# Cross-attention and feed-forward block on one Trainium2 core: the softmax of the first two tiles placed ahead of V and U, and the centring of Wq moved to ScalarE and GpSimd

## The chip, the core and the metric

The kernel runs on one core of a Trainium2 chip. The metric is the device time of one execution in microseconds (us), lower is better. One profiled execution gives the trace; its span runs from the first to the last instruction, and the execution's own time lies somewhat above it. The engines are TensorE (PE; its weight loads are PEld), VectorE (DVE), ScalarE (ACT), GpSimd (POOL) and SyncE (SP), which only issues transfers here.

## What is computed

```python
# x (2, 1024, 256), ctx (2, 77, 192); 8 heads of 128
def xattn(x, ctx):                      # x is layer-normalised first
    q = (x @ Wq) * SCALE; k = (ctx @ Wk) * SCALE; v = ctx @ Wv   # per head
    attn = softmax(q k^T)               # 1024 x 77 per head
    return (attn v) @ Wo + bo
def ffn(x):                             # x is layer-normalised first
    shared = square(relu(x @ Ws1)) @ Ws2
    prob = trunc(softmax(top2(x @ Wr)))     # 8 experts, two chosen
    return shared + routed(x, W1, W2, prob)
x = x + xattn(layernorm(x), ctx)
x = x + ffn(layernorm(x))
```

A truncated softmax weight is 0 unless one of the two is 1, so the routed experts count only where a gate opens. The kernel tests this at its end and runs them in a branch that is not taken with these inputs.

## The kernel before, in words

**Folding.** The kernel multiplies weights with the context first. K and V (transposed, per head) come from the context by `context_main` (rows 0 to 127 of the 192) and `context_tails` (the other 64). Per head h, A = Wq_h K_h^T (256 x 154, both batches) and UT = (V_h Wo_h)^T. Scores of a tile of 128 rows are then x A for 8 heads x 77 keys, in two halves of 308 columns, and attention's output is P U, where U is UT turned. The layer norm's mean is taken out of Wq ahead of time: each row of Wq^T has its mean over the 256 inputs subtracted (`centre_wq`, lines 1039 to 1047), and the row's standard deviation enters as the scale of the exponential. In the same way `wsr_c` is Ws1 and Wr with their mean (`wmean_bank`) subtracted.

**Precision.** A float32 matmul of scores or attention is made of three products of high and low parts (`three`, lines 420 to 422). The high part is a rounded copy by ScalarE (`a_hi`, `u_hi`, `pt_hi`) or GpSimd (`xt_hi`); the low part is a subtraction by VectorE (`a_lo`, `u_lo`, `pt_lo`) or GpSimd (`xt_lo`). So before attention of a tile its probabilities are normalised (GpSimd, `normalise`), turned by TensorE (`transposes`), copied by ScalarE and subtracted by VectorE.

**Tiles.** There are 16 tiles of 128 rows; even ones belong to batch 0, odd ones to batch 1 (`par`). Every engine has its own instruction stream, written by hand, with counting semaphores between them. `step(t)` on TensorE is: turn tile t's probabilities, scores of tile t+2, turn the attended rows of t-1, feed-forward products of t-1 and t-2, attention of t. On ScalarE it is: copies of the turned blocks, the second half of the exponentials of t+1, relu, the first half of those of t+2. Steps 2 to 13 are loops (`pairs`); step 1 and all before are written out.

**The opening.** TensorE makes K, then A (`make_a`) with V's products between the heads, scores of tiles 0 and 1, UT (`make_ut`), U (`make_u` in four parts of two chunks and a last chunk of 104 rows, `last_bank`), part of the scores of tile 2, turns tile 0, the rest of tile 2's scores and one of four parts of tile 3's, attention of tile 0, step 1. VectorE centres Wq two heads at a time (sum, scale, subtract), subtracts A's low parts (`lo_of_a`), makes statistics, maxima and their negation for the exponentials, copies UT, and subtracts U's low parts. ScalarE copies K, A, V, then makes 16 exponentials of tiles 0 and 1 (one per head, lines 691 to 699), then copies U and tile 0's turned probabilities, then tile 2's.

**PSUM.** There are eight banks: `s_ps` four (two per parity, for scores), `g_ps` two (turned blocks), `o_ps`, `f_ps`. In the opening, K and A use the four of `s_ps` (A twice over: head h+4 waits until head h is split), V, UT and U use the other four (`once_banks`), and `last_bank` is the fourth of `s_ps`. Tile 0 is turned into `g_ps` and so waits for U's first parts to be split (line 577 on).

**Transfers.** All loads are issued from SyncE in one queue, in the order: context and Wk, Wq pairs 0 and 1, first half of Wv, Wq pairs 2 and 3, second half of Wv, x_t and x of the first four tiles, Ws1 and Wr, Wo, bo, Ws2, the other x_t and x.

## Time and profile before

| | us |
|---|---|
| median of the three runs shown | 118.31 |
| lowest, highest | 118.0, 119.46 |
| the profiled execution's own time | 118.02 |
| its span | 116.2 |
| busy: TensorE, VectorE, ScalarE, GpSimd | 109.9, 90.1, 84.6, 63.4 |

The granted clock of TensorE is 0.993 of full speed over the span. A row of a timeline gives start and length in us, engine, line, operation, what it writes and reads with shapes, and in square brackets how long the engine had been idle before it and what ended that. Float32 matmuls show as two rows each, transposes and float32r matmuls as one.

### The profile page before, as it was taken

To read this page: it belongs to the slowest core of one execution; us is meant where nothing else is said; L and a number is where in the kernel's file an instruction comes from. 1 tells how busy PE (TensorE), PEld (TensorE's weight loads), DVE (VectorE), ACT (ScalarE), POOL (GpSimd) and SP (SyncE) were. 2 spreads that over 40 slices of the span, in tenths; PEclk is the share of its full clock that TensorE was granted. 3 is DMA by queue.
4 is the path that set the end of the run, shared out by engine and by line. 5 is a ranking of instruction groups with operands and counts; after the bars stand their busy time and mean duration, and the time that the engine had idled before them with its cause. 6 is when DMAs were issued, how large, how long until landed. Compare 5 with 4: busy or idle time off the path is not lost.

```text
span 116.2 us, 3116 instructions
## 1 busy us (share of the span) xinstructions
PE 109.9 (95%) x854; PEld 106.1 (91%) x854; DVE 90.1 (77%) x351; ACT 84.6 (73%) x345; POOL 63.4 (55%) x103
## 2 busy tenths in 40 slices
PE   6997999999899989999999999999999999989981
PEld 6986989998798889999999999999999999979970
DVE  0039987996978597887979797887979696798963
ACT  4016544899659879898989899898989789994320
POOL 2000173359616965786676578657746865369250
PEclk9999999999999999999999999999999999999997
DMA  3799999994000100022005000400400050031033
GB/s 65 249 343 351 352 338 351 351 348 159 0 8 0 71 19 0 6 102 78 0 0 181 0 0 36 145 0 0 177 4 0 0 181 6 0 120 60 29 140 102
DMA packets 11815, 12.70 MB, mean 109 GB/s; under 512 B 1056, under 2 KB 10272, under 8 KB 11808
## 3 DMA queue, kind: packets, MB, share of 16 engines
q1 hardware_dynamic: 11520, 12.36, 32.1%
q10 hardware_dynamic: 288, 0.26, 0.7%
q8 instruction: 3, 0.05, 0.2%
q14 instruction: 4, 0.03, 0.1%
HBM read 8.42 MB, written 2.10 MB: 91 GB/s over the span
## 4 chain that ended last, share of the span: by engine, by line
PE 67%; DVE 12%; ACT 10%; DMA 4%; issue 3%; SPq 2%; DVEq 0%; ACTq 0%
ACT probs L695 8%; PE o_ps L420 7%; PE o_ps L422 7%; PE o_ps L421 7%; PE s_ps L420 6%; PE s_ps L422 6%; PE s_ps L421 6%; PE g_ps L479 5%; PE f_ps L509 4%; DMA wqt_sb<-in_wq_t 4%; PE s_ps L414 3%; PE g_ps L492 2%; PE f_ps L420 2%; DVE row_max L911 2%; DVE u_lo L1032 2%
## 5 line engine op out<-in xcount | busy, mean ns | idle before, releaser
L695 ACT ACTIVATE probs<-s_ps,neg_max,rstd 128x77 f32<-128x77 f32 x128 | 51.5, 424 | 8.8 <-DVE neg_max L919 8.7
L815 POOL TENSOR_TENSOR probs<-probs,recip 128x308 f32<-128x308 f32 x31 | 21.7, 701 | 23.7 <-DVE recip L925 23.7
L695 ACT ACTIVATION_READ_ACCUMULATOR probs<-s_ps,neg_max,rstd 128x1 f32 x128 | 27.3, 213 | 0.0
L420 PE MATMUL o_ps<-u_hi,pt_hi 128*128 128x256 f32 (+1 forms) x80 | 22.7, 284 | 0.9 <-DVE pt_lo L933 0.5
L422 PE MATMUL o_ps<-u_lo,pt_hi 128*128 128x256 f32 (+1 forms) x80 | 22.3, 279 | 0.0
L421 PE MATMUL o_ps<-u_hi,pt_lo 128*128 128x256 f32 (+1 forms) x80 | 22.3, 279 | 0.0
L420 PE MATMUL s_ps<-a_hi,xt_hi 128*128 128x308 f32 x64 | 22.0, 344 | 0.0
L422 PE MATMUL s_ps<-a_lo,xt_hi 128*128 128x308 f32 x64 | 19.5, 304 | 0.0
L421 PE MATMUL s_ps<-a_hi,xt_lo 128*128 128x308 f32 x64 | 19.4, 303 | 0.0
L420 PEld LDWEIGHTS o_ps<-u_hi,pt_hi 128*128 128x128 f32 (+1 forms) x80 | 15.0, 188 | 1.5 <-DVE pt_lo L933 0.9
L421 PEld LDWEIGHTS o_ps<-u_hi,pt_lo 128*128 128x128 f32 (+1 forms) x80 | 15.1, 189 | 0.0
L422 PEld LDWEIGHTS o_ps<-u_lo,pt_hi 128*128 128x128 f32 (+1 forms) x80 | 15.0, 188 | 0.0
L952 DVE TENSOR_TENSOR x_tr<-o_ps,xb_sb 128x256 f32<-128x256 f32 x14 | 5.9, 423 | 9.7 <-PE o_ps L422 9.7
L911 DVE TENSOR_REDUCE row_max<-s_ps 128x8 f32<-128x616 f32 x16 | 12.4, 775 | 0.7 <-PE s_ps L422 0.7
L797 POOL TENSOR_TENSOR xt_lo<-xt_sb,xt_hi 128x256 fp32r<-128x256 f32 x16 | 11.6, 728 | 2.2 <-POOL xt_hi L795 0.2
L420 PEld LDWEIGHTS s_ps<-a_hi,xt_hi 128*128 128x128 f32 x64 | 12.1, 189 | 0.2 <-issue 0.2
L421 PEld LDWEIGHTS s_ps<-a_hi,xt_lo 128*128 128x128 f32 x64 | 12.2, 190 | 0.0
L422 PEld LDWEIGHTS s_ps<-a_lo,xt_hi 128*128 128x128 f32 x64 | 12.0, 188 | 0.0
L819 POOL TENSOR_TENSOR xb_sb<-x_sb,bo_sb 128x256 f32<-128x256 f32 x16 | 11.8, 739 | 0.0
L479 PE MATMUL g_ps<-ident,probs 128*128 128x128 f32 x76 | 11.5, 273 | 0.2 <-POOL probs L815 0.2
L937 DVE TENSOR_TENSOR pt_lo<-g_ps,pt_hi 128x512 fp32r<-128x512 f32 x14 | 9.6, 687 | 1.0 <-ACT pt_hi L681 0.6
L479 PEld LDWEIGHTS g_ps<-ident,probs 128*128 128x128 f32 x76 | 8.7, 140 | 0.5 <-POOL probs L815 0.5
(163 smaller groups left out, 253.4 us busy)
## 6 DMA issues: line engine op xcount, KB each, us to landing
xt_sb<-in_x_t SPq DMA_DIRECT2D x8, 256.0 KB, 6.4
x_sb<-in_x SPq DMA_DIRECT2D x8, 256.0 KB, 6.5
x_sb<-x_tr SPq DMA_DIRECT2D x7, 256.0 KB, 2.3
out<-y_sb SPq DMA_DIRECT2D x6, 256.0 KB, 2.3
wqt_sb<-in_wq_t SPq DMA_DIRECT2D x4, 256.0 KB, 5.1
wo_sb<-in_wo SPq DMA_DIRECT2D x1, 1024.0 KB, 8.8
...
```

The lines of the kernel that those rows point to most:

```text
L420: pe.matmul(out_ap, hi, rhs_hi, start=first, stop=False)
L421: pe.matmul(out_ap, lo, rhs_hi, start=False, stop=False)
L422: return pe.matmul(out_ap, hi, rhs_lo, start=False, stop=last)
L479: mm = pe.transpose(to, probs[:, par, c * P:(c + 1) * P], ident[:, :])
L509: mm = pe.matmul(f_ps[:, D:D + NL], g_sb[:, c * P:(c + 1) * P], wsr_c[:, c, :], start=c == 0, stop=c == DCH - 1)
L695: e = act.activation(probs[:, par, h * TK:(h + 1) * TK], s_ps[:, 2 * par + half, (h - half * H // 2) * TK:(h - half * H // 2 + 1) * TK], A ...
L797: pool.tensor_tensor(xt_lo[:, par, :, :], src, xt_hi[:, par, :, :].bitcast(F32), ALU.subtract).then_inc(xt_ready, 1)
L815: pool.tensor_tensor(rows, rows, recip[:, par, hs].unsqueeze(2).broadcast_to([P, H // 2, TK]), ALU.mult).then_inc(probs_ready, 1)
L819: pool.tensor_tensor(xb_sb[:, par, :], x_sb[:, t, :], bo_sb[:, :], ALU.add).then_inc(xb_ready, 1)
L911: dve.tensor_reduce(row_max[:, par, :].rearrange("p (i h) -> p i h", i=2), s_ps[:, 2 * par:2 * par + 2, 0:HALF].rearrange("p i (h k) -> p ...
L937: dve.tensor_tensor(pt_lo[:, 0:PB], g_ps[:, 0:PB], pt_hi[:, 0:PB].bitcast(F32), ALU.subtract).then_inc(ptlo_ready, 1)
L952: dve.tensor_tensor(x1_of(t, par), o_ps[:, 0:D], xb_sb[:, par, :], ALU.add).then_inc(x1_ready, 1)
```

## The change

- **Wq.** VectorE keeps only the sum and the scale, now by -1/256 (`mean_of_wq`; heads 0 and 1 apart, then pairs). The mean is added by ScalarE for heads 0, 4 and 5 (an Identity with a bias, `centre_wq`) and by GpSimd for heads 1, 2 and 3, 6 and 7 (three instructions), each with a semaphore of its own.
- **A** has eight banks instead of four twice over, so no head waits for a split.
- **Order.** Scores of tiles 0 and 1 come ahead of V, scores of tile 2 ahead of UT. ScalarE makes tile 0's exponentials ahead of V's copies, and tile 2's first half ahead of all of U's.
- **Tile 0** is turned ahead of U, into `s_ps` banks 0 and 2 instead of `g_ps`. Its probabilities and tile 1's have a buffer of their own, `probs_first`, so that tile 2's exponentials don't wait for it.
- **U** is made in the order (0,0), (1,0), (0,1), (1,1) of (batch, half). Attention of tiles 0 and 1 waits for each part of U where it is used, not for all at once.
- **Tile 3's scores**: half of them stand ahead of attention of tile 0 (before: one part of four), the other half in step 1.
- **Transfers.** Wv goes behind x, Ws1 and Wr.

```diff
+        probs_first = sb("probs_first", [P, 2, KC * P])
...
-        a_banks = [s_ps[:, i, :] for i in range(4)] * 2
+        a_banks = [s_ps[:, i, :] for i in range(4)] + once_banks
         u_bank = {(0, 0): once_banks[0], (0, 1): once_banks[1], (1, 0): once_banks[2], (1, 1): once_banks[3]}
         last_bank = s_ps[:, 3, :]
-        wmean_bank = once_banks[2]
+        wmean_bank = once_banks[0]
...
+        def probs_of(t):
+
+            return probs_first if isinstance(t, int) and t < 2 else probs
+
+        def first_one(t):
+            return isinstance(t, int) and t == 0
+
+        def main_turned(t):
+            return s_ps[:, 0, 0:PB] if first_one(t) else g_ps[:, 0:PB]
+
+        def last_turned(t, n):
+            return s_ps[:, 2, 0:n] if first_one(t) else g_ps[:, LO:LO + n]
+
         def pt_bank(t, par, c):
 
+            if first_one(t):
+                return s_ps[:, 0, c * P:(c + 1) * P]
...
-            load_wq(0)
-            load_wq(1)
-            load_wv(0)
-            load_wq(2)
-            load_wq(3)
-            load_wv(1)
+            for i in range(4):
+                load_wq(i)
...
             sp.dma_start(wsr_sb[:, :, 0:FE], ws1.rearrange("(c p) f -> p c f", p=P)).then_inc(wsr_in, 16)
             sp.dma_start(wsr_sb[:, :, FE:NL], wr.rearrange("(c p) e -> p c e", p=P)).then_inc(wsr_in, 16)
+            load_wv(0)
+            load_wv(1)
             sp.dma_start(wo_sb[:, :, :], wo.rearrange("(h p) d -> p h d", p=P)).then_inc(wo_in, 16)
...
-            def make_a(heads):
-                for h in heads:
-                    pe.wait_ge(wq_ready, h // 2 + 1)
+            def make_a():
+                for h in range(H):
+                    if h in (0, 4, 5):
+                        pe.wait_ge(wqact_ready, (1, 2, 3)[(0, 4, 5).index(h)])
+                    else:
+                        pe.wait_ge(wqpool_ready, {1: 1, 2: 2, 3: 2, 6: 3, 7: 3}[h])
                     if h < H // 2:
                         pe.wait_ge(kt_copied, h + 1)
-                    else:
-                        pe.wait_ge(alo_ready, h - H // 2 + 1)
...
-                if isinstance(t, int) and t < 2:
-                    pe.wait_ge(ulo_ready[t], 2)
-                    pe.wait_ge(ulastlo_ready, 1)
                 pe.wait_ge(ptlo_ready, pt_count(t, 0))
                 for c in range(KC):
+                    if isinstance(t, int) and t < 2 and c % 2 == 0:
+                        if c < KC - 1:
+                            pe.wait_ge(ulo_ready[t], c // 2 + 1)
+                        else:
+                            pe.wait_ge(ulastlo_ready, 1)
...
                     if isinstance(t, int) and t == 1:
-                        parts = ((0, 1), (1, 0), (1, 1))
+                        pe.wait_ge(ulastlo_ready, 1)
+                        scores(t + 2, par, ((1, 0),))
+                        transposes_x1(t, par, mm)
+                        scores(t + 2, par, ((1, 1),))
                     else:
-                        parts = ((0, 0), (0, 1), (1, 0), (1, 1))
-                    scores(t + 2, par, parts[:1])
-                    transposes_x1(t, par, mm)
-                    scores(t + 2, par, parts[1:])
+                        scores(t + 2, par, ((0, 0),))
+                        transposes_x1(t, par, mm)
+                        scores(t + 2, par, ((0, 1), (1, 0), (1, 1)))
...
-            make_a(range(0, 4))
-            context_main(wv_sb, 0, wv_in[0], once_banks)
-            make_a(range(4, 6))
-            context_main(wv_sb, 1, wv_in[1], once_banks)
-            make_a(range(6, H))
-            context_tails(wv_sb, once_banks, vt_ready)
-            scores(0, 0)
+            make_a()
+            scores(0, 0, ((0, 0), (0, 1)))
             pe.wait_ge(wsr_in, 32)
-            pe.wait_ge(vt_copied, 3)
+            pe.wait_ge(alo_ready, H // 2 + 1)
             for c in range(DCH):
                 mm = pe.matmul(wmean_bank[:, 0:NL], mean_of[:, :], wsr_sb[:, c, :], start=c == 0, stop=c == DCH - 1)
             mm.then_inc(wmean_ready, 1)
+            scores(0, 0, ((1, 0), (1, 1)))
             scores(1, 1)
+            pe.wait_ge(wsr_ready, 1)
+            for i in range(2):
+                context_main(wv_sb, i, wv_in[i], once_banks)
+            context_tails(wv_sb, once_banks, vt_ready)
+            scores(2, 0)
             make_ut()
             pe.wait_ge(const_ready, 4)
-            for b, i in ((0, 0), (0, 1), (1, 0), (1, 1)):
+            pe.wait_ge(exp_done, 5)
+            transposes_x1(0, 0, transposes(0, 0))
+            for b, i in ((0, 0), (1, 0), (0, 1), (1, 1)):
                 make_u(b, i)
-            pe.wait_ge(exp_done, 4)
             for b in range(B):
                 mm = u_chunk(b, KC - 1, last_bank[:, b * D:(b + 1) * D])
             mm.then_inc(ulast_ready, 1)
-            scores(2, 0, ((0, 0), (0, 1)))
-            pe.wait_ge(ulo_ready[0], 2)
-            transposes_x1(0, 0, transposes(0, 0))
-            scores(2, 0, ((1, 0), (1, 1)))
-            scores(3, 1, ((0, 0),))
+            pe.wait_ge(ptlo_last, 1)
+            scores(3, 1, ((0, 0), (0, 1)))
...
+            def centre_wq(h, count):
+                act.wait_ge(wqs, count)
+                act.activation(wqt_sb[:, h, :], wqt_sb[:, h, :], ACT.Identity, bias=wq_mean[:, 1, h:h + 1]).then_inc(wqact_ready, 1)
+
             for g in range(H // 2):
                 act.wait_ge(kt_ready, g + 1)
                 act.activation(kt_sb[:, 2 * g:2 * g + 2, :].rearrange("p h n -> p (h n)"), s_ps[:, g, 0:2 * BK],
                                ACT.Copy, scale=SCALE2).then_inc(kt_copied, 1)
+                if g == 0:
+                    centre_wq(0, 2)
+            centre_wq(4, 8)
+            centre_wq(5, 8)
...
+            exps(0, 0, 0)
+            exps(0, 0, 1)
             for g in range(H // 2):
                 act.wait_ge(vt_ready, g + 1)
                 act.activation(vt_sb[:, 2 * g:2 * g + 2, :].rearrange("p h n -> p (h n)"), once_banks[g][:, 0:2 * BK],
                                ACT.Copy).then_inc(vt_copied, 1)
-            exps(0, 0, 0)
-            exps(0, 0, 1)
             exps(1, 1, 0)
             exps(1, 1, 1)
-            for b, i in ((0, 0), (0, 1), (1, 0)):
+            exps(2, 0, 0)
+            copy_transposes(0, 0)
+            for b, i in ((0, 0), (1, 0), (0, 1)):
                 hi_of_u(b, i)
             act.wait_ge(ulast_ready, 1)
             act.activation(u_hi[0:KLAST, :, KC - 1, :], last_bank[0:KLAST, :].rearrange("p (b d) -> p b d", b=B),
                            ACT.Copy).then_inc(ulasthi_ready, 1)
             hi_of_u(1, 1)
-            copy_transposes(0, 0)
             act.wait_ge(ws2_in, 16)
             act.activation(ws2_hi[:, :], ws2_sb[:, :], ACT.Copy).then_inc(ws2hi_ready, 1)
-            exps(2, 0, 0)
...
+            for first, heads, count in ((1, 1, 4), (2, 2, 6), (6, 2, 10)):
+                hs = slice(first, first + heads)
+                pool.wait_ge(wqs, count)
+                pool.tensor_tensor(wqt_sb[:, hs, :], wqt_sb[:, hs, :],
+                                   wq_mean[:, 1, hs].unsqueeze(2).broadcast_to([P, heads, D]), ALU.add).then_inc(wqpool_ready, 1)
             turned_x(0, 0)
             turned_x(1, 1)
-            for t in range(3):
-                rstd_first(t)
+            rstd_first(0)
+            rstd_first(1)
             turned_x(2, 0)
+            rstd_first(2)
+            rstd_first(3)
...
+            dve.memset(probs_first[:, :, HK:KC * P], 0.0).then_inc(fill_ready, 1)
+
+            def mean_of_wq(i, first, heads, count):
+                hs = slice(first, first + heads)
                 dve.wait_ge(wq_in[i], 16)
                 dve.tensor_reduce(wq_mean[:, 0, hs], wqt_sb[:, hs, :], X, ALU.add).then_inc(wqs, 1)
-                dve.wait_ge(wqs, 2 * i + 1)
-                dve.tensor_scalar(wq_mean[:, 1, hs], wq_mean[:, 0, hs], 1.0 / D, None, ALU.mult).then_inc(wqs, 1)
-                dve.wait_ge(wqs, 2 * i + 2)
-                dve.tensor_tensor(wqt_sb[:, hs, :], wqt_sb[:, hs, :],
-                                  wq_mean[:, 1, hs].unsqueeze(2).broadcast_to([P, 2, D]), ALU.subtract).then_inc(wq_ready, 1)
+                dve.wait_ge(wqs, count)
+                dve.tensor_scalar(wq_mean[:, 1, hs], wq_mean[:, 0, hs], -1.0 / D, None, ALU.mult).then_inc(wqs, 1)
...
-            for i in range(3):
-                centre_wq(i)
-            lo_of_a(0)
-            lo_of_a(1)
-            centre_wq(3)
-            for h in range(2, H):
+            mean_of_wq(0, 0, 1, 1)
+            mean_of_wq(0, 1, 1, 3)
+            for i in range(1, 4):
+                mean_of_wq(i, 2 * i, 2, 2 * i + 3)
+            for h in range(H):
                 lo_of_a(h)
-            dve.wait_ge(x_in[0], 32)
-            all_stats_x(0, 0)
-            all_stats_x(1, 1)
-            maxima(0, 0)
-            neg_maxima(0, 0)
             dve.wait_ge(wmean_ready, 1)
             dve.tensor_tensor(wsr_c[:, :, :], wsr_sb[:, :, :],
                               wmean_bank[:, 0:NL].unsqueeze(1).broadcast_to([P, DCH, NL]), ALU.subtract).then_inc(wsr_ready, 1)
-            all_stats_x(2, 0)
+            dve.wait_ge(x_in[0], 32)
+            all_stats_x(0, 0)
+            maxima(0, 0)
+            neg_maxima(0, 0)
+            all_stats_x(1, 1)
             maxima(1, 1)
             neg_maxima(1, 1)
+            all_stats_x(2, 0)
+            all_stats_x(3, 1)
+            reciprocals(0, 0, 0)
+            reciprocals(0, 0, 1)
+            maxima(2, 0)
+            neg_maxima(2, 0)
...
-            reciprocals(1, 1, 0)
-            reciprocals(1, 1, 1)
-            for b, i in ((0, 0), (0, 1), (1, 0)):
+                    reciprocals(1, 1, 1)
+            lo_of_transposes(0, 0)
+            lo_of_last(0, 0)
+            reciprocals(2, 0, 0)
+            for b, i in ((0, 0), (1, 0), (0, 1)):
                 lo_of_u(b, i)
             dve.wait_ge(ulasthi_ready, 1)
             dve.tensor_tensor(u_lo[0:KLAST, :, KC - 1, :], last_bank[0:KLAST, :].rearrange("p (b d) -> p b d", b=B),
                               u_hi[0:KLAST, :, KC - 1, :].bitcast(F32), ALU.subtract).then_inc(ulastlo_ready, 1)
+            dve.wait_ge(x_in[1], 32)
             lo_of_u(1, 1)
-            dve.wait_ge(x_in[1], 32)
-            lo_of_transposes(0, 0)
-            lo_of_last(0, 0)
-            maxima(2, 0)
-            neg_maxima(2, 0)
-            all_stats_x(3, 1)
+            all_stats_x(4, 0)
             attended(0, 0)
-            all_stats_x(4, 0)
-            reciprocals(2, 0, 0)
```

The three places in the order that follow show instructions as they stand in the built programs, without time.

TensorE, from K's tails on, before; `kt_sb` with `wqt_sb` is an A product, `wv_sb` a V product, `a_hi` with `xt_hi` the scores.

```order
L401 MATMUL s_ps<-ctx_sb,wk_sb 128x154 x8
L414 MATMUL s_ps<-kt_sb,wqt_sb 128x154 x8
L391 MATMUL g_ps<-ctx_sb,wv_sb 128x154 x4
L414 MATMUL s_ps<-kt_sb,wqt_sb 128x154 x4
L391 MATMUL o_ps<-ctx_sb,wv_sb 128x154 x2
L391 MATMUL f_ps<-ctx_sb,wv_sb 128x154 x2
L414 MATMUL s_ps<-kt_sb,wqt_sb 128x154 x4
L401 MATMUL g_ps<-ctx_sb,wv_sb 128x154 x4
L401 MATMUL o_ps<-ctx_sb,wv_sb 128x154
L401 MATMUL f_ps<-ctx_sb,wv_sb 128x154
```

After, the same place.

```order
L415 MATMUL s_ps<-ctx_sb,wk_sb 128x154 x8
L429 MATMUL s_ps<-kt_sb,wqt_sb 128x154 x8
L429 MATMUL g_ps<-kt_sb,wqt_sb 128x154 x4
L429 MATMUL o_ps<-kt_sb,wqt_sb 128x154 x2
L429 MATMUL f_ps<-kt_sb,wqt_sb 128x154 x2
L435 MATMUL s_ps<-a_hi,xt_hi 128x308
L436 MATMUL s_ps<-a_hi,xt_lo 128x308
L437 MATMUL s_ps<-a_lo,xt_hi 128x308
```

V's products have left A's stage, A's later heads go to `g_ps`, `o_ps` and `f_ps`, and the scores of tile 0 follow at once; the mean product of Ws1 and Wr stands between their two halves, behind the rows shown.

GpSimd, from its last constant to the first row scale, before.

```order
L832 AFFINE_SELECT ident<-ident 128x128
L792 CAST xt_hi<-xt_sb 128x256
L797 TENSOR_TENSOR xt_lo<-xt_sb,xt_hi 128x256
L792 CAST xt_hi<-xt_sb 128x256
L797 TENSOR_TENSOR xt_lo<-xt_sb,xt_hi 128x256
L804 TENSOR_TENSOR rstd<-var,pow_neg 128x1 x3
```

After.

```order
L857 AFFINE_SELECT ident<-ident 128x128
L862 TENSOR_TENSOR wqt_sb<-wqt_sb,wq_mean 128x256
L862 TENSOR_TENSOR wqt_sb<-wqt_sb,wq_mean 128x512 x2
L817 CAST xt_hi<-xt_sb 128x256
L822 TENSOR_TENSOR xt_lo<-xt_sb,xt_hi 128x256
L817 CAST xt_hi<-xt_sb 128x256
L822 TENSOR_TENSOR xt_lo<-xt_sb,xt_hi 128x256
L829 TENSOR_TENSOR rstd<-var,pow_neg 128x1 x2
```

The subtraction of Wq's mean, 256 columns once and 512 twice, now stands ahead of the split of x (`xt_hi`, `xt_lo`) of tiles 0 and 1.

TensorE, from U (`ident` with `ut_sb`) on, before.

```order
L443 MATMUL g_ps<-ident,ut_sb 128x128 x8
L443 MATMUL o_ps<-ident,ut_sb 128x128 x4
L443 MATMUL f_ps<-ident,ut_sb 128x128 x4
L443 MATMUL s_ps<-ident,ut_sb 104x128 x4
L420 MATMUL s_ps<-a_hi,xt_hi 128x308
L421 MATMUL s_ps<-a_hi,xt_lo 128x308
L422 MATMUL s_ps<-a_lo,xt_hi 128x308
L420 MATMUL s_ps<-a_hi,xt_hi 128x308
L421 MATMUL s_ps<-a_hi,xt_lo 128x308
L422 MATMUL s_ps<-a_lo,xt_hi 128x308
L479 MATMUL g_ps<-ident,probs 128x128 x5
```

After; `probs_first` is tile 0.

```order
L493 MATMUL s_ps<-ident,probs_first 128x128 x5
L457 MATMUL g_ps<-ident,ut_sb 128x128 x4
L457 MATMUL o_ps<-ident,ut_sb 128x128 x4
L457 MATMUL g_ps<-ident,ut_sb 128x128 x4
L457 MATMUL f_ps<-ident,ut_sb 128x128 x4
L457 MATMUL s_ps<-ident,ut_sb 104x128 x4
L435 MATMUL s_ps<-a_hi,xt_hi 128x308
L436 MATMUL s_ps<-a_hi,xt_lo 128x308
L437 MATMUL s_ps<-a_lo,xt_hi 128x308
```

Tile 0 is turned ahead of U and into `s_ps`, and no part of tile 2's scores stands here any more; what follows U is tile 3's first half.

## Rows read from the trace of the kernel before

**Rows 1.** The page: busy time of TensorE; GB/s moved in 40 slices.
```profile
PE 109.9 (95%) x854; PEld 106.1 (91%) x854; DVE 90.1 (77%) x351; ACT 84.6 (73%) x345; POOL 63.4 (55%) x103
...
GB/s 65 249 343 351 352 338 351 351 348 159 0 8 0 71 19 0 6 102 78 0 0 181 0 0 36 145 0 0 177 4 0 0 181 6 0 120 60 29 140 102
```

**Rows 2.** Busy time by stretch: start:end, length, then each engine.
```profile
core 0: us, PE busy (x) PEld busy (x) DVE busy (x) ACT busy (x) POOL busy (x), PEclk, DMA share, GB/s
...
8.74:17.70 8.96, 8.18 (x65) 7.48 (x65) 8.45 (x19) 4.74 (x13) 2.68 (x4) 1.00 1.06 348
17.70:21.66 3.96, 3.96 (x31) 3.96 (x29) 2.96 (x11) 1.75 (x8) 1.12 (x2) 1.00 1.10 352
21.66:25.85 4.19, 4.19 (x34) 4.19 (x33) 4.02 (x13) 4.19 (x23) 2.53 (x5) 1.00 1.10 348
25.85:28.31 2.46, 2.32 (x22) 2.09 (x21) 1.35 (x5) 2.46 (x11) 2.32 (x5) 1.00 0.71 226
...
33.47:38.13 4.66, 4.59 (x37) 4.35 (x36) 4.21 (x20) 4.14 (x20) 2.47 (x5) 1.00 0.01 2
38.13:44.30 6.17, 5.63 (x45) 5.19 (x43) 4.44 (x23) 5.56 (x25) 4.97 (x8) 1.00 0.11 42
44.30:96.52 52.22, 52.22 (x422) 52.09 (x421) 43.75 (x187) 46.32 (x201) 34.86 (x56) 1.00 0.14 51
```

**Rows 3.** Timeline of TensorE: start, length, line, operation, [idle before <-releaser].
```profile
9.31 1.31 PE L414 MATMUL s_ps<-kt_sb,wqt_sb 128*128 128x154 f32 x8 [0.58 <-ACT kt_sb L720]
10.84 1.31 PE L414 MATMUL s_ps<-kt_sb,wqt_sb 128*128 128x154 f32 x8 [0.21 <-DVE wqt_sb L1046]
11.99 1.21 PE L391 MATMUL g_ps<-ctx_sb,wv_sb 128*128 128x154 f32 x8
...
16.45 0.80 PE L401 MATMUL g_ps<-ctx_sb,wv_sb 64*128 64x154 f32 x8
...
31.68 0.35 PE L420 MATMUL o_ps<-u_hi,pt_hi 128*128 128x256 f32 x1 [0.41 <-DVE pt_lo L937]
...
42.08 0.38 PE L420 MATMUL f_ps<-ws_hi,pt_hi 128*128 128x256 f32 x1 [0.31 <-DVE pt_lo L943]
```

**Rows 4.** The chain that ended last, in order of time: start, length.
```profile
20.88 6.46 ACT probs L695 x32
27.34 0.50 ACT u_hi L716
...
33.23 1.70 ACT probs L695 x8
```

**Rows 5.** Timeline of VectorE.
```profile
7.64 0.69 DVE L1042 TENSOR_REDUCE wq_mean<-wqt_sb 128x2 f32<-128x512 f32 x1 [6.57 <-DMA wqt_sb<-in_wq_t]
8.36 0.17 DVE L1044 TENSOR_SCALAR wq_mean<-wq_mean 128x2 f32<-128x2 f32 x1
8.56 0.69 DVE L1046 TENSOR_TENSOR wqt_sb<-wqt_sb,wq_mean 128x512 f32<-128x512 f32 x1
...
20.61 0.23 DVE L919 TENSOR_SCALAR neg_max<-row_max,rstd 128x8 f32<-128x8 f32 x1
...
27.86 1.29 DVE L1032 TENSOR_TENSOR u_lo<-g_ps,u_hi 128x512 fp32r<-128x512 f32 x2 [0.31 <-ACT u_hi L716]
...
36.99 0.76 DVE L911 TENSOR_REDUCE row_max<-s_ps 128x8 f32<-128x616 f32 x1
```

**Rows 6.** Timeline of ScalarE.
```profile
8.24 1.39 ACT L720 ACTIVATE kt_sb<-s_ps 128x308 f32<-128x308 f32 x4 [6.22 <-PE s_ps L401]
```

**Rows 7.** Groups of instructions by form, ScalarE and GpSimd.
```profile
L750 ACT ACTIVATE y_part<-f_ps,rvar 128x256 f32<-128x256 f32 x1 | 0.5, 473 | 1.8 <-PE f_ps L620 1.8
...
L815 POOL TENSOR_TENSOR probs<-probs,recip 128x308 f32<-128x308 f32 x31 | 21.7, 701 | 23.7 <-DVE recip L925 23.7
...
L872 POOL TENSOR_TENSOR probs<-probs,recip 128x154 f32<-128x154 f32 x1 | 0.4, 442 | 0.1
```

**Rows 8.** Timeline of GpSimd.
```profile
14.07 0.89 POOL L792 CAST xt_hi<-xt_sb 128x256 fp32r<-128x256 f32 x1 [12.50 <-DMA xt_sb<-in_x_t]
```

35 lines of the change are left out of this document (15 added, 20 removed).

## The prediction

> **What bounds the kernel now.** I read the page's first part, then busy time by stretch. TensorE (PE) is busy 95% of the span [rows 1], and from 44.30 to 96.52 us, ten steps of the loop, it has no idle time: 52.22 of 52.22 us, 5.22 a step, granted clock 1.00 [rows 2]. The change touches nothing there, so it can gain only before 44.30 us, by letting the loop begin earlier. In the stretches before it the reader should compare length and PE busy: 8.96 to 8.18, 2.46 to 2.32, 4.66 to 4.59, 6.17 to 5.63 [rows 2], and a wait of 0.41 at 31.68 [rows 3]. Together they leave 1.94 us idle. A modelled matmul outlasts its pitch (eight rows of L391 begin 1.05 apart from the next group and show 1.21), so a gap shows about 0.2 short; with some seven gaps and switches I estimate the true loss at 3.2 us. That is all there is to win.
>
> PE's timeline names the gaps: the first A product waits 0.58 for K's copy and for centred wq, the third another 0.21, and attention of tile 0 waits 0.41 for pt_lo [rows 3]. The chain of waits tells why the last is late: 6.46 us of exponentials of tiles 0 and 1 on ScalarE, then the copies of U (0.50 to the next link), then U's low halves on VectorE, and tile 2's exponentials only at 33.23 [rows 4]. At 42.08 PE waits again (0.31) for tile 2's last low half [rows 3], which follows tile 3's negated maximum.
>
> **The opening, step by step.** VectorE now takes 0.69 for a two-head sum, 0.17 for the scale, 0.69 for the subtraction [rows 5]; the subtraction leaves it. The first pair is halved: a sum of 256 lies between 0.17 and 0.69, and I take 0.42. So head 0's mean stands at 7.64 + 0.45 + 0.17 = 8.26, head 1's at 8.81. Each later pair follows 0.82 after (0.69 + 0.17, less overlap): 9.63, 10.45, 11.27, provided wq has landed; it has, because only the V weights leave the queue ahead of it.
>
> ScalarE's first K copy begins at 8.24, four take 1.39 [rows 6]. Head 0 is centred behind the first. The nearest row is y_part's 128x256 Identity with a pointer, 0.473 [rows 7]; K's copy of 308 columns, 1.39 less the overlaps or about 0.43, bounds it below, so it matters little. It ends near 9.03, and A's first head starts at 9.08 against 9.31.
>
> GpSimd's subtraction is not in the trace for this shape. The broadcast multiply takes 0.701 for 308 columns and 0.442 for 154 [rows 7]: 1.68 ns a column on 0.18. So 256 cost 0.61 and 512 cost 1.04. For 512 the bounds are 0.70 (no dearer than 308) and 1.40 (twice that). Head 1 is ready at 8.87 + 0.61 = 9.48, heads 2 and 3 at 9.68 + 1.04 = 10.72, heads 6 and 7 at 11.32 + 1.04 = 12.36. PE finishes head 1 at about 10.1, so **a new gap of 0.7 us** stands before head 2. Heads 4 and 5 are ScalarE's, done by 11.34. Six heads at half of 1.05 (eight matmul rows, two heads [rows 3]) take 3.15: A ends at 10.80 + 3.15 = 13.95. ScalarE's a_hi copies start late, at 11.25, but in eight separate banks, and have caught up by head 6; a_lo of head 7 ends near 14.9. GpSimd splits x of tile 0 after its centring: x_t now lands some 2.2 us before 14.07 [rows 8], since 768 KB of V weights no longer stand before it at 351 GB/s [rows 1], so this starts at 12.36 and is ready between 13.6 and 14.1.
>
> The Trainium skill ("GPSIMD Engine Reference", Engine selection) speaks against this edit: for an elementwise op on two inputs it advises VectorE, GpSimd being about 2x slower. By twice VectorE's 0.69 the 512-column op would be 1.38 and the gap 1.0, and the sum below would come out 0.3 smaller; the rows' slope for a broadcast operand gives 1.04.
>
> **From A to the loop.** Stage lengths are those of the windows [rows 2], in the new order: switch 0.1, scores of tiles 0 and 1 with the mean product 3.96 (to 18.0); V, 16 rows at 2.10 and tails at 1.25 as before (16.45 to 17.70 [rows 2, 3]), with 0.1 to 21.45; scores of tile 2, 1.79 with its switch, to 23.25; UT 4.19, to 27.45; tile 0 turned 0.5; U 2.32 (its 0.14 of idle time gone) to 30.25; half of tile 3's scores 0.9, to 31.15; attention of tile 0, 33.47 - 31.68 = 1.79 and a switch, to 33.0. Before it ended at 33.47, with one part of tile 3's scores less behind it (0.43). Step 1 was 4.66 with 0.07 idle; without that part it is 4.2, so it ends at 37.2 against 38.13: **0.9 gained**.
>
> Every cover must hold. ScalarE: the negated maximum of tile 0 now starts about 17.55 against 20.61 [rows 5] (mean product 15.35, wsr_c 0.4, statistics 0.75, maximum 0.9). Exponentials: 8 heads at 6.46/16 = 0.40 from 17.83 to 21.0, V's four copies 1.3, eight more to 25.4, tile 2's first half to 27.0. PE asks for that at 27.45: 0.45 to spare. VectorE copies UT till 27.98, then pt_lo of tile 0, then five U parts at 0.60 each (1.29 for two, overlapping [rows 5]): pt_lo from 28.64, parts from 29.53, the last-chunk part done by 32.0. Attention asks for it at chunk 4, near 32.6: 0.6 to spare. Its first chunks need the (0,0) part at 30.1. If this cover fails, each microsecond late costs one.
>
> Step 1 also waits for attended rows and their copy as before. ScalarE is free when tile 1 is turned (33.4), where before it copied only at 34.93, behind 1.70 of tile 2's exponentials [rows 4]. This lead of 1.4 runs through pt_lo, the maximum of tile 3 (36.99 before [rows 5], now 35.6), its negation and exponentials. So row 42.08 of PE [rows 3], whose release hangs on that chain, moves to about 40.7, and PE alone reaches it at 40.4. **Gain at loop entry 1.3 to 1.4**; I take 1.3. The loop repeats its 5.22 a step, and the end is unchanged.
>
> The profiled execution took 118.02 for a span of 116.2 (1.8 around it). 118.02 - 1.3 = 116.7; the median of the shown runs is 0.3 above it (118.31). I say 116.8.
>
> **Rivals.** *A: the late gain fails.* ScalarE or VectorE in 18 to 32 us has 0.5 us of spare only; an exponential start half a microsecond later, plus attention waiting for U's low halves, uses it up. Then only the A start and the 0.43 of scores remain, or nothing: 117.8. For it: VectorE gets two statistics blocks and two more splits in a dense queue. Against: its stretches are no fuller than 4.0 of 4.19 before. Chance 0.20.
>
> *B: more is won.* If the GpSimd op costs 0.70 the new gap is half, and if the switches I kept at 0.1 vanish, 2.4 or more of the 3.2 us goes: 115.6. Against: the gap before head 2 stays even at 0.70, as the second pair's mean is not there before 9.63. Chance 0.12.
>
> *C: slower, GpSimd as the new bound.* Its queue holds two 512-column ops, then the split of x, 1.25, that the first scores need. It ends at 9.68 + 2X + 1.25, against 14.05 needed. X = 1.56 is free; at X = 2.2 the whole 1.3 is gone; at X = 3.5 scores start 3.9 late: 120.6. For it: an add along a row-wise constant of 256 columns, in place, has no row of its own, and the engine's queue is where a dear op would delay both A and the scores. Against: the multiply of the same form follows its columns (0.442 and 0.701 [rows 7]). Chance 0.04.
>
> *D: the clock.* Through gaps of 0.58 and 0.21 near 9 to 11 us the granted clock stayed 1.00 (2.4 GHz) [rows 2, 3]. Now the gaps are 0.5 and 0.7, closer together. If it fell to the lower level, 1.2 GHz, through the A stage, its last six heads would take 3.15 us more, and the scores behind them some of theirs: 119.9. The Trainium skill ("TensorE: Matmul & The Clock Gate", What's actually happening) has the gate fall back to half rate when the engine has been idle. By that rule these gaps could bring it about; the trace, with gaps of like size at a granted clock of 1.00, does not bear it out. Chance 0.03.
>
> That the change does not do what it says: the order of both programs shows the scores ahead of V, so no.
>
> **How the numbers follow.** The forecast has 0.61: 116.8, own range 116.2 to 117.5, from the GpSimd price (0.70 gives 0.35 more, 1.40 takes 0.35) and the covers' half microsecond. A to 117.8 and part of B are taken in: 115.7 to 118.3. Faster by over 2% is below 115.9, most of B: 0.11. Slower by over 2% is above 120.7: part of C and D, 0.03. The rest is within 2%, about what a measurement of this kernel can tell from no change.
>
> **What would show it.** Right: A's first head near 9.1, one gap of about 0.7 before head 2, A done near 14.0, exponentials from about 17.8, no PE gap over 0.3 from 14 to 33, the loop's step still 5.22, and PE's fourth tile beginning at 43.0 against 44.3. Wrong: a GpSimd subtraction over 1.5 us; PE waiting for exponentials before tile 0 is turned, or for u_lo in attention of tile 0; a granted clock under 1.00 before 20 us; a loop step that differs.

## The result, and the profile after

| | before | after |
|---|---|---|
| median, same batch, us | 118.55 (118.0 to 119.46, 4 runs) | 117.24 (116.98 to 117.36, 4 runs) |
| ratio after / before | | 0.987, 95% interval 0.9831 to 0.9908 |
| profiled execution, its span | 118.02, 116.2 | 117.36, 115.5 |

The forecast was 116.8 (115.7 to 118.3), no difference over 2%. The kernel is 1.3 us faster by the medians, and the whole interval lies below 1. The two profiled executions differ by only 0.7; the experiments say why. (Two more batches below give 0.9866 and 0.9853.)

From the page of the changed kernel, the parts that answer to [rows 1], and its chain of waits by engine:

```profile
PE 109.2 (95%) x854; PEld 105.9 (92%) x854; DVE 87.8 (76%) x350; ACT 85.5 (74%) x348; POOL 65.5 (57%) x106
...
PE 80%; DVE 7%; DMA 4%; ACT 2%; SPq 2%; issue 2%; POOL 1%; DVEq 0%; ACTq 0%
```

The same line of the page before:

```profile
PE 67%; DVE 12%; ACT 10%; DMA 4%; issue 3%; SPq 2%; DVEq 0%; ACTq 0%
```

TensorE carries 80% of the chain where it carried 67%, ScalarE 2% where it had 10%: the run of exponentials of [rows 4] is no longer on it.

Busy time by stretch of the changed kernel, cut where the stages change (columns as in [rows 2]): A; scores of tiles 0 and 1; V; scores of tile 2; UT; tile 0 turned and U; attention of tile 0; step 1; ten steps of the loop.

```profile
9.59:14.63 5.04, 4.61 (x33) 4.27 (x33) 4.44 (x11) 3.95 (x12) 3.88 (x6) 1.00 1.08 361
14.63:18.64 4.01, 4.01 (x32) 4.01 (x31) 3.50 (x11) 0.77 (x3) 1.53 (x3) 1.00 1.10 352
18.64:22.07 3.43, 3.43 (x34) 3.11 (x32) 3.03 (x13) 3.43 (x18) 2.44 (x5) 1.00 1.10 348
22.07:23.87 1.80, 1.80 (x15) 1.80 (x14) 0.00 (x0) 1.80 (x9) 1.80 (x4) 1.00 1.10 347
23.87:28.06 4.19, 4.19 (x35) 4.19 (x33) 3.87 (x11) 3.96 (x20) 1.79 (x4) 1.00 0.89 283
28.06:30.71 2.65, 2.65 (x28) 2.65 (x26) 2.02 (x6) 2.01 (x5) 1.87 (x3) 1.00 0.04 15
31.64:33.42 1.78, 1.78 (x17) 1.78 (x16) 1.78 (x4) 0.74 (x2) 0.96 (x2) 1.00 0.04 9
33.42:37.66 4.24, 4.19 (x34) 3.84 (x33) 3.83 (x18) 3.12 (x13) 1.86 (x4) 1.00 0.00 0
43.60:95.80 52.20, 52.20 (x422) 52.14 (x421) 43.76 (x187) 46.21 (x200) 34.78 (x56) 1.00 0.14 51
```

From 14.63 us on TensorE is busy for the whole of every stretch up to step 1; the loop's step is still 5.22.

TensorE's timeline of the changed kernel, its only rows with a wait from 6 to 46 us:

```profile
7.77 1.32 PE L415 MATMUL s_ps<-ctx_sb,wk_sb 64*128 64x154 f32 x16 [0.59 <-DMA wk_sb<-in_wk_p]
9.59 1.46 PE L429 MATMUL s_ps<-kt_sb,wqt_sb 128*128 128x154 f32 x8 [0.50 <-ACT wqt_sb L737]
11.48 1.32 PE L429 MATMUL s_ps<-kt_sb,wqt_sb 128*128 128x154 f32 x8 [0.43 <-POOL wqt_sb L862]
41.40 0.38 PE L435 MATMUL f_ps<-ws_hi,pt_hi 128*128 128x256 f32 x1 [0.26 <-DVE pt_lo L974]
```

Before there were five such places: the four of [rows 3] and this one.

```profile
38.74 0.55 PE L479 MATMUL g_ps<-ident,probs 128*128 128x128 f32 x3 [0.23 <-POOL probs L815]
```

It and the wait of 0.41 before attention of tile 0 are gone, the gap before head 2 is new. VectorE's timeline, where the change put the sums and scales of Wq (L1074 sums, L1076 scales); the last row is a small VectorE operation of the statistics, for later:

```profile
8.39 0.42 DVE L1074 TENSOR_REDUCE wq_mean<-wqt_sb 128x1 f32<-128x256 f32 x1 [7.25 <-DMA wqt_sb<-in_wq_t]
8.84 0.15 DVE L1076 TENSOR_SCALAR wq_mean<-wq_mean 128x1 f32<-128x1 f32 x1
...
10.14 0.17 DVE L1076 TENSOR_SCALAR wq_mean<-wq_mean 128x2 f32<-128x2 f32 x1
10.21 0.68 DVE L1074 TENSOR_REDUCE wq_mean<-wqt_sb 128x2 f32<-128x512 f32 x1
10.93 0.52 DVE L1076 TENSOR_SCALAR wq_mean<-wq_mean 128x2 f32<-128x2 f32 x1
...
20.83 0.15 DVE L921 TENSOR_SCALAR var<-mv 128x1 f32<-128x1 f32 x1
```

GpSimd's and ScalarE's timelines of the same stretch, the centring itself:

```profile
9.59 0.61 POOL L862 TENSOR_TENSOR wqt_sb<-wqt_sb,wq_mean 128x256 f32<-128x256 f32 x1 [8.03 <-DVE wq_mean L1076]
10.39 1.04 POOL L862 TENSOR_TENSOR wqt_sb<-wqt_sb,wq_mean 128x512 f32<-128x512 f32 x1 [0.18 <-DVE wq_mean L1076]
```

```profile
9.03 0.51 ACT L737 ACTIVATE wqt_sb<-wqt_sb,wq_mean 128x256 f32<-128x256 f32 x1
...
18.51 0.42 ACT L712 ACTIVATE probs_first<-s_ps,neg_max,rstd 128x77 f32<-128x77 f32 x1 [3.15 <-DVE neg_max L950]
```

The first sum of Wq starts at 8.39, where it was 7.64 [rows 5]: the weights landed 0.75 us later in this execution, and A's first head follows (9.59 against 9.31).

### The profile page after: what moved, and what is told of

Read it like the earlier page. It is cut to its first block, busy times and chain, and to the rows that moved or that the text cites. A ratio compares the mean times of both kernels' runs of the same rounds, so it can differ in the third digit from the quotient of the medians.

```text
span 115.5 us, 3118 instructions
## 1 busy us (share of the span) xinstructions
PE 109.2 (95%) x854; PEld 105.9 (92%) x854; DVE 87.8 (76%) x350; ACT 85.5 (74%) x348; POOL 65.5 (57%) x106
## 4 chain that ended last, share of the span: by engine, by line
PE 80%; DVE 7%; DMA 4%; ACT 2%; SPq 2%; issue 2%; POOL 1%; DVEq 0%; ACTq 0%
PE o_ps L435 8%; PE o_ps L437 8%; PE o_ps L436 8%; PE s_ps L435 7%; PE s_ps L437 7%; PE s_ps L436 7%; PE g_ps L493 6%; PE f_ps L523 4%; DMA wqt_sb<-in_wq_t 4%; PE g_ps L506 3%; PE f_ps L435 2%; PE g_ps L449 2%; ACT probs L712 1%; PE f_ps L437 1%; PE f_ps L436 1%
## 5 line engine op out<-in xcount | busy, mean ns | idle before, releaser
L712 ACT ACTIVATE probs<-s_ps,neg_max,rstd 128x77 f32<-128x77 f32 x112 | 45.2, 425 | 4.0 <-DVE neg_max L950 4.0
L840 POOL TENSOR_TENSOR probs<-probs,recip 128x308 f32<-128x308 f32 x27 | 18.9, 701 | 23.4 <-DVE recip L956 23.3
L712 ACT ACTIVATION_READ_ACCUMULATOR probs<-s_ps,neg_max,rstd 128x1 f32 x112 | 24.0, 214 | 0.0
L493 PE MATMUL g_ps<-ident,probs 128*128 128x128 f32 x66 | 10.1, 273 | 0.0
L968 DVE TENSOR_TENSOR pt_lo<-g_ps,pt_hi 128x512 fp32r<-128x512 f32 x13 | 8.9, 687 | 1.1 <-ACT pt_hi L698 0.6
L698 ACT ACTIVATE pt_hi<-g_ps 128x512 fp32r<-128x512 f32 x13 | 7.8, 601 | 1.7 <-PE g_ps L493 1.7
```

What stands on the lines that cost most here:

```text
L493: mm = pe.transpose(to, probs_of(t)[:, par, c * P:(c + 1) * P], ident[:, :])
L698: act.activation(pt_hi[:, 0:PB], main_turned(t), ACT.Copy).then_inc(pthi_ready, 1)
L712: e = act.activation(probs_of(t)[:, par, h * TK:(h + 1) * TK], s_ps[:, 2 * par + half, (h - half * H // 2) * TK:(h - half * H // 2 + 1) * TK],
L840: pool.tensor_tensor(rows, rows, recip[:, par, hs].unsqueeze(2).broadcast_to([P, H // 2, TK]), ALU.mult).then_inc(probs_ready, 1)
L968: dve.tensor_tensor(pt_lo[:, 0:PB], main_turned(t), pt_hi[:, 0:PB].bitcast(F32), ALU.subtract).then_inc(ptlo_ready, 1)
```

## The experiments

The landing is the moment when a transfer's data have arrived. To take it out I also read, in each trace, the distance from A's first matmul to the first matmul of the shared expert's second layer on tile 0 (row 42.08 of before, [rows 3]; row 41.40 of after), and call it D. Behind that row each trace goes on for the same 74.0 to 74.5 us. D is 42.08 - 9.31 = 32.77 before and 41.40 - 9.59 = 31.81 after.

**1. Both kernels again.** No edit.

> The kernel before once more, to see how far one profile differs from the next. Theory 1: the first pair of Wq (VectorE's first sum at 7.64 us in the profile of before, 8.39 in that of after) lands at times that vary from run to run by some 0.7 us whatever the kernel; then this profile can show 8.4 and a span near 116.9. Theory 2: the changed transfer order itself delays the first pair; then this profile shows 7.6 again.

> The changed kernel once more. Theory 1 (landing varies by run): ratio to before 0.987 to 0.991 by many runs, first sum at 7.6 or 8.4 by chance. Theory 2 (the order delays it): first sum at 8.4 again, while before stays at 7.6. In both the gap before head 2 is there and a two-head add on GpSimd takes 1.04.

> The changed kernel again, as the twin of the others of this batch: 0.987 of the kernel before, within 0.982 to 0.991; the gap before head 2 at 0.43 us, VectorE's scale beside GpSimd's 512-column add at 0.52.

| | median, us | ratio to before | first Wq sum | A begins | D |
|---|---|---|---|---|---|
| before_again | 118.96 | 0.9993 (0.9958 to 1.0029) | 8.80 | 10.47 | 33.13 |
| after_again | 117.52 | 0.9866 (0.9819 to 0.9913) | 8.52 | 9.72 | 31.78 |
| after_third | 117.08 | 0.9853 (0.9814 to 0.9891) | 8.09 | 9.76 | 31.36 |

In VectorE's timeline of before_again the same kernel gets Wq 1.16 us later than in [rows 5]:

```profile
8.80 0.69 DVE L1042 TENSOR_REDUCE wq_mean<-wqt_sb 128x2 f32<-128x512 f32 x1 [7.73 <-DMA wqt_sb<-in_wq_t]
```

So 7.64 was an early landing, the earliest of all fourteen traces of this document, and the trace behind the forecast was a lucky one. The order of the transfers doesn't explain it: the first sum starts between 7.64 and 8.80 with the order of before and between 7.78 and 8.52 with that of the change. D is 32.95 before (mean of two) and 31.65 after (mean of three): 1.3 us.

D has a flaw of its own: A's first head waits for K as well as for Wq, and where K is late, as in after_third, D comes out short. Counted from the first Wq sum instead, D's row comes 34.44 and 34.80 us later before, and 33.01, 32.98 and 33.03 after. That is the steadier measure, and it says 1.4 to 1.8. The medians of these two batches say 1.5 and 1.65 (before: 119.02 and 118.73), the first batch says 1.3. The 0.43 before head 2 and the scale of 0.52 come again in after_again; in after_third A began so late (K's tails at 8.06) that GpSimd's add was nearly done, and the gap is below what the profile lists.

**2. Centring back on VectorE, all else changed** (dve_centres), **and the centring alone in the kernel before** (before_centre).

```diff
-            centre_wq(4, 8)
-            centre_wq(5, 8)
...
-            for first, heads, count in ((1, 1, 4), (2, 2, 6), (6, 2, 10)):
...
+            for i in range(3):
+                centre_pair(i)
+            lo_of_a(0)
+            lo_of_a(1)
+            centre_pair(3)
+            for h in range(2, H):
+                lo_of_a(h)
```

Here `centre_pair` is a pair's sum, scale and add, all on VectorE. before_centre makes the opposite edit in the kernel before, whose order, banks and transfers stay.

> The changed kernel with the whole centring of Wq back on VectorE (three pairs, A's first two low halves, the fourth pair), all else as changed. Theory (the opening is a chain through the centring and A's split): a pair costs 0.69 + 0.17 + 0.69, so A ends about 1.1 us later than with the change and the last a_lo near 17.5 instead of 15.9; scores and the loop begin 1.3 to 1.6 later, and the kernel is at 0.998 to 1.003 of the kernel before: the new order alone wins nothing. Rival (the order of the softmax is what wins, the centring only helps): at most 0.5 slower than the changed kernel, 0.991.

> The kernel before with the centring of Wq alone moved to ScalarE and GpSimd. Theory (A and V share TensorE before the first scores, and GpSimd's 1.04 puts a gap of its own before head 2): 0 to 0.4 us faster than before, 0.997 to 1.000. Rival (the centring is the whole gain): 1.3 us faster, 0.989.

dve_centres: 119.14 us, ratio 1.0036 (1.0004 to 1.0068), D 33.54. TensorE's timeline, its waits in A behind the first head:

```profile
11.15 1.31 PE L426 MATMUL s_ps<-kt_sb,wqt_sb 128*128 128x154 f32 x8 [0.21 <-DVE wqt_sb L1076]
12.91 1.32 PE L426 MATMUL g_ps<-kt_sb,wqt_sb 128*128 128x154 f32 x8 [0.44 <-DVE wqt_sb L1076]
15.39 0.79 PE L426 MATMUL o_ps<-kt_sb,wqt_sb 128*128 128x154 f32 x4 [1.16 <-DVE wqt_sb L1076]
```

The new order by itself wins nothing. First scores come at 16.44 instead of 14.63, exponentials at 20.32 instead of 18.51: the last pair stands on VectorE behind two a_lo splits, and nothing now lies between A and the scores to cover it. About 0.4 us of this isn't the queue: x lands earlier in the changed order, GpSimd splits it beside VectorE's centring, and two scales take 0.40 and 0.35 instead of 0.17 (more on this in the last section). Centring the last pair ahead of the splits was not tried, so what is shown is that the order gains nothing with VectorE's queue as it was.

before_centre: 118.11 us, ratio 0.995 (0.9913 to 0.9987), about 0.55 us gained, a little more than I expected. Counted from the first Wq sum (7.92) A begins 1.20 later, against 1.67 before, but D's row comes 34.53 later, against 34.44 and 34.80: the trace doesn't place the gain. D is 33.33, not shorter: here A waits again, for its reused bank (0.53 at 13.90, released by a_lo), and the 0.41 before attention stays. So neither part gives the 1.3 us or more by itself: the centring opens the way, the order uses it.

**3. Heads shared out evenly** (even_odd, even_odd_again): ScalarE centres heads 0, 2, 4, 6, GpSimd 1, 3, 5, 7, one at a time.

```diff
-for first, heads, count in ((1, 1, 4), (2, 2, 6), (6, 2, 10)):
+for first, heads, count in ((1, 1, 4), (3, 1, 6), (5, 1, 8), (7, 1, 10)):
```

> The changed kernel with ScalarE centring heads 0, 2, 4, 6 and GpSimd heads 1, 3, 5, 7, one head per instruction. If the opening is bound by the centring of heads 2 and 3 (1.04 on GpSimd), the gap before head 2 falls from about 0.85 between matmuls to 0.3, all of the chain to the loop moves with it, and the time falls by 0.4 to 0.6 us against the changed kernel. Rival: the opening is bound by ScalarE's a_hi copies and exponentials; then A ends earlier but the loop begins at the same time and the total is the same within 0.1.

> ScalarE centres the even heads and GpSimd the odd ones, one head at a time, again and beside the changed kernel. Theory 1 (the gap before head 2 and what follows from it is the whole gain): 0.3 to 0.5 us below the changed kernel, f_ps row that much nearer to the first Wq sum. Theory 2 (the 0.75 us of the first time held a gain that the gap does not account for): 0.7 us or more below it, and the trace shows TensorE faster in a second place. Rival: no difference in time, the first result was the spread of the transfers.

116.77 us, ratio 0.9824 (0.9778 to 0.9871), D 31.23; again 116.46, 0.9804 (0.9766 to 0.9842), D 31.34. It is 0.75 and 0.62 us below the changed kernel of its batch and faster than both kernels. TensorE's timeline of even_odd has all of A's first four heads in one row, without the wait for GpSimd:

```profile
9.28 2.66 PE L426 MATMUL s_ps<-kt_sb,wqt_sb 128*128 128x154 f32 x16 [0.38 <-ACT wqt_sb L734]
```

Against after and after_again D is 0.4 to 0.6 shorter, which is the gap. Against after_third it is the same, because there A's first head waited for K (K's tails at 8.06, against 7.46 in even_odd_again), and what it waited was no longer waited before head 2. Counted from the first Wq sum, D's row comes 32.58 and 32.55 later, against 33.01, 32.98 and 33.03: the gap costs 0.45 in every trace of the changed kernel, after_third included. That is 0.45 of the 0.75 and 0.62. In the second pair Wq landed 0.1 earlier (7.99, 8.09), which accounts for most of the rest of the profiled executions' 0.61; what the medians have beyond the 0.45 is not placed further. The 0.62 lies between the 0.3 to 0.5 of my first theory and the 0.7 of my second. The edit also changes two things at once, the grain of GpSimd's adds and who centres head 2, and no run parts them.

**4. Transfers in the order of before** (wv_early): V's first weights go out behind Wq's second pair.

```diff
-            for i in range(4):
-                load_wq(i)
+            load_wq(0)
+            load_wq(1)
+            load_wv(0)
+            load_wq(2)
+            load_wq(3)
+            load_wv(1)
...
-            load_wv(0)
-            load_wv(1)
```

> The changed kernel with the transfers in the order of before (Wv halves among the Wq pairs). Theory: x_t of the first tiles lands 2.2 us later, near 14.1, the split x of tile 0 is ready near 15.3 instead of 14.5, and the first scores start 0.7 later: 0.7 us slower than the changed kernel, about half of the whole gain gone. Rival: the transfers' place is hidden behind A, within 0.2 of the changed kernel.

118.2 us, ratio 0.9934 (0.9904 to 0.9965): 0.7 slower than after_again, the size expected. TensorE's timeline of the profiled execution:

```profile
12.08 1.32 PE L431 MATMUL s_ps<-kt_sb,wqt_sb 128*128 128x154 f32 x8 [1.28 <-POOL wqt_sb L864]
...
16.21 0.41 PE L437 MATMUL s_ps<-a_hi,xt_hi 128*128 128x308 f32 x1 [0.37 <-POOL xt_lo L824]
```

x costs 0.37. The larger wait comes from Wq itself: VectorE's sums of pairs 1 and 2 start at 10.02 and 11.67, each after 0.76 of waiting for its transfer. Only the later of the two stands behind V in the queue, and in scale_psum, with no V there, the earlier one waited too (0.38). The profiled execution took 119.0, the longest of the twelve. So my cost for the order of the transfers was right in sum, and this trace has it in another place; where it lies in the median execution isn't shown.

**5. How much cover ScalarE has** (act_plus3): three spare copies, 1.55 us, ahead of tile 2's exponentials.

```diff
+            for i in range(3):
+                act.wait_ge(spare_done, i)
+                act.wait_ge(kt_copied, 1)
+                act.activation(spare[:, :], kt_sb[:, 0:2, :].rearrange("p h n -> p (h n)"), ACT.Copy).then_inc(spare_done, 1)
             exps(2, 0, 0)
```

> The changed kernel with three useless 128x308 copies on ScalarE, each waiting for the one ahead of it, between tile 1's exponentials and tile 2's: about 1.3 us of ScalarE time. In the profile of the changed kernel tile 2's first half of exponentials ends 0.1 to 0.3 us ahead of TensorE's turning of tile 0. Theory (ScalarE is nearly critical there): 0.9 to 1.2 us slower than the changed kernel, with TensorE waiting before the turned tile 0. Rival (0.5 us or more of cover, and more slack behind it): at most 0.5 slower.

```profile
28.96 0.74 PE L495 MATMUL s_ps<-ident,probs_first 128*128 128x128 f32 x5 [1.06 <-issue]
```

TensorE's row says it: 1.55 added, a wait of 1.06 before tile 0 is turned. The cover (how late ScalarE could be before TensorE waits) was 0.49 or, as a gap shows 0.2 short, nearer 0.3; ScalarE ends tile 2's first half at 27.8 in after and is asked at 28.06. The time is 119.23, ratio 1.0036 (1.0004 to 1.0068), 1.95 above the mean of the changed kernel's three medians (117.28) and more than the 0.9 to 1.2 I expected. The trace places 1.3 of it (D 32.35, 0.7 longer; A 0.3 later; 0.3 behind D's row). Another 0.35 lies outside the span: time less span is 2.12 to 2.23 in its six executions and 1.76 to 1.93 in all others of this document, and why is not known. The last 0.3 is not placed.

**6. V ahead of the first scores again** (v_first): V, its copies and its transfers first, UT ahead of tile 2's scores, tile 0's reciprocals and tile 2's maxima in or behind VectorE's copies of UT, centring as changed.

```diff
+            for i in range(2):
+                context_main(wv_sb, i, wv_in[i], once_banks)
+            context_tails(wv_sb, once_banks, vt_ready)
             scores(0, 0, ((0, 0), (0, 1)))
...
-            for i in range(2):
-                context_main(wv_sb, i, wv_in[i], once_banks)
-            context_tails(wv_sb, once_banks, vt_ready)
-            scores(2, 0)
             make_ut()
+            scores(2, 0)
```

> The changed kernel with V's products, their copies and their transfers ahead of the first scores again, UT ahead of tile 2's scores, and tile 0's reciprocals in VectorE's copies of UT as before; centring, A's banks, tile 0's turning and all behind it as changed. Theory (what the new order buys is the early start of the exponentials): they start about 3.5 us later, near 22, and tile 2's first half ends 2 us or more after TensorE needs tile 0 turned: 1.5 to 2.5 us slower than the changed kernel, so slower than before. Rival (TensorE's work is the same sum in any order and no engine is late): within 0.4 of the changed kernel.

124.68 us (122.94 to 126.33), ratio 1.044 (1.038 to 1.0501). TensorE's timeline of its profiled execution (122.94):

```profile
15.57 1.31 PE L405 MATMUL g_ps<-ctx_sb,wv_sb 128*128 128x154 f32 x8 [1.03 <-DVE a_lo L1082]
26.66 1.32 PE L449 MATMUL g_ps<-vt_sb,wo_sb 128*128 128x154 f32 x8 [1.30 <-DVE ut_sb L1105]
33.72 0.73 PE L493 MATMUL s_ps<-ident,probs_first 128*128 128x128 f32 x5 [3.00 <-issue]
```

Exponentials start at 23.00 instead of 18.51, but that is not what TensorE pays the 3.00 for. ScalarE's timeline and VectorE's:

```profile
31.92 0.42 ACT L713 ACTIVATE probs<-s_ps,neg_max,rstd 128x77 f32<-128x77 f32 x1 [2.46 <-DVE neg_max L951]
```

```profile
30.75 0.80 DVE L943 TENSOR_REDUCE row_max<-s_ps 128x8 f32<-128x616 f32 x1 [1.13 <-PE s_ps L437]
```

ScalarE is through with tile 1 at 29.46 and idle for 2.46 until tile 2's maximum, and VectorE idle for 1.13 until tile 2's scores, which end just ahead of the turn. So the long wait is the time from tile 2's scores to its exponentials, laid open because this edit puts UT ahead of those scores. In the changed kernel UT (4.19) stands between and covers it. The run shows that place of UT to be needed. It doesn't show what an early start of the exponentials is worth; act_plus3 does, where ScalarE's delay alone reaches TensorE. It isn't the kernel before either, where tile 2's exponentials aren't due before tile 0 is turned. Of the 1.5 to 2.5 that I expected my reason was wrong, and two waits were missing: V needs the banks of A's later heads, held until a_lo has read them (1.03), and UT's copies stand on VectorE behind the statistics of tiles 2 and 3, to 26.13 (1.30).

**7. Tile 0 turned behind U** (u_first): in the changed order, on TensorE, ScalarE and VectorE.

```diff
-transposes_x1(0, 0, transposes(0, 0))
 for b, i in ((0, 0), (1, 0), (0, 1), (1, 1)):
     make_u(b, i)
...
+transposes_x1(0, 0, transposes(0, 0))
```

> Tile 0 is turned behind U and its last chunk again (TensorE, ScalarE and VectorE, other banks and all else as changed). Theory 1 (the late gain comes from turning first, so that the copies of the probabilities do not stand behind those of U): ScalarE would end U's five copies at about 31.3 and the turned tile at 32.1, VectorE pt_lo at about 33.3, so TensorE waits before tile 3's scores and begins attention of tile 0 near 34.2 instead of 31.6: 2.0 to 2.7 us slower than the changed kernel. Rival (the same work in another order on engines with idle time, so the place of the turn is nearly free): at most 0.5 us slower.

120.08 us (119.76 to 121.4), ratio 1.0116 (1.0063 to 1.0169): 3.0 above after_third of its batch. TensorE's timeline and the stretches of its profiled execution (121.29):

```profile
33.20 0.62 PE L435 MATMUL s_ps<-a_hi,xt_hi 128*128 128x308 f32 x1 [2.64 <-DVE pt_lo L974]
...
34.91 0.41 PE L435 MATMUL o_ps<-u_hi,pt_hi 128*128 128x256 f32 x1
```

```profile
31.00:32.00 1.00, 0.00 (x0) 0.00 (x0) 0.76 (x2) 1.00 (x4) 0.00 (x0) 1.00 0.00 0
32.00:33.00 1.00, 0.00 (x0) 0.00 (x0) 1.00 (x3) 0.10 (x1) 0.73 (x1) 0.92 0.02 8
33.00:34.00 1.00, 0.80 (x3) 0.80 (x4) 0.88 (x5) 0.00 (x0) 0.69 (x2) 0.50 0.00 0
34.00:35.00 1.00, 1.00 (x6) 1.00 (x5) 0.00 (x0) 0.00 (x0) 0.85 (x3) 0.50 0.00 0
...
36.50:37.00 0.50, 0.50 (x7) 0.50 (x6) 0.00 (x0) 0.00 (x0) 0.00 (x0) 1.00 0.00 0
```

The copies stand behind U's as expected: ScalarE ends pt_hi at 31.79, VectorE pt_lo at 33.15, and TensorE waits 2.64. Counted from A's first matmul the scores of tile 3 come 2.86 late (33.20 - 9.22 against 30.71 - 9.59), and as much counted from the first Wq sum, against after_third too (33.20 - 8.02 against 30.41 - 8.09). That is close to the 3.0 of the medians; I had expected 2.0 to 2.7. The place of the turn is not free; the late gain needs it.

**8. The long scale** (scale_psum): the sums land in PSUM, so the scale no longer reads SBUF.

```diff
-dve.tensor_reduce(wq_mean[:, 0, hs], wqt_sb[:, hs, :], X, ALU.add)
+dve.tensor_reduce(o_ps[:, hs], wqt_sb[:, hs, :], X, ALU.add)
```

> The sums of Wq land in PSUM and VectorE's scale reads them there, so that it is no SBUF to SBUF operation any more. Theory 1 (the scale was held because it and GpSimd's add both need what VectorE and GpSimd share on the SBUF side): the scale beside GpSimd's 512-column add takes 0.15 to 0.25 us instead of 0.52, although the add still runs. Rival (the scale waits for something else at that place, a landing or a semaphore): 0.5 us again. The time is that of the changed kernel within 0.4 us either way, since nothing waited for the scale.

117.39 us, ratio 0.9875 (0.9809 to 0.9941). Every scale took 0.16, but Wq's second and third pair landed late here (0.38 and 0.70 of waiting), and no scale came beside a GpSimd add (add at 10.29 to 11.33, scale at 11.63). It tells the theories apart in nothing; only the forecast for the time, within 0.4 of the changed kernel, held.

## Why the prediction was right, point by point

- **Where time can be won.** Right: the loop's step stayed 5.22 and everything behind D's row 74.1 us. All of the gain is ahead of it.
- **The opening.** ScalarE's head costs 0.51 (0.473 taken), the sum of 256 took 0.42, GpSimd's adds 0.61 and 1.04, as the slope of [rows 7] gave to the digit. By twice VectorE's 0.69, as the Trainium skill would have it ("GPSIMD Engine Reference", Engine selection), the larger would be 1.38; the trace does not agree. Head 2 began 1.89 after head 0, 0.84 above the pitch of 1.05, with 0.67 forecast. A's first head was to start at 9.08 and started at 9.59, since Wq landed 0.75 later: this term was bound to one execution's landing.
- **From A to the loop.** Lengths, with the forecast behind each. Scores of tiles 0 and 1 4.01 (4.06 with the switch), V 3.43 (3.45), tile 2 1.80 (1.8), UT 4.19 (4.2), tile 0 turned and U 2.65 (2.8), attention of tile 0 1.78 (1.85), step 1 4.24 (4.2). From A to D's row the forecast has 40.7 - 9.08 = 31.6; the three traces show 31.4 to 31.8. Counted from the first Wq sum, which the forecast left at 7.64, it has 40.7 - 7.64 = 33.06, and the three traces show 32.98 to 33.03. Existing stages moved whole kept their lengths.
- **The covers.** ScalarE's was 0.45 in the forecast and 0.26 by the profile; act_plus3 shows it at 0.3 to 0.5. It held, but narrowly. VectorE's held: the last-chunk part ends at 32.67 in after (32.0 forecast), and its first use is near 33.1, 0.4 later (0.6 forecast).
- **The late gain.** u_first shows the mechanism: turned behind U, its copies wait for U's, 3.0 us. dve_centres shows what the forecast did not price: without the centring moved the order gains nothing. The forecast counted the two as terms of one sum; they only pay together.
- **The sum.** 1.3 forecast for D's row; 1.43 between the two traces when both are counted from the first Wq sum. By the medians 1.31, 1.5 and 1.65 in three batches, so that the first agrees to the digit is partly luck. The two profiled executions alone say 0.7, because the one of before had the early landing. The time itself was 116.8 forecast and 117.24 measured: the forecast went down from that early execution (118.02, the lowest of the four) and added 0.1 where it had read 0.3 to the median. One slip changes nothing: 1.94 and seven times 0.2 are 3.3, not 3.2.
- **Rivals.** A (late gain fails) did not occur. B (more is won) did not, but even_odd took another 0.6 to 0.75 at the gap that B named. C needed an add over 1.56. D did not occur in this kernel, but u_first shows that a clock fall is real at a longer wait.
